# Where the fourth head's softmax denominator is summed: GpSimd adds in place of TensorE products with ones

## What is computed

```python
q = (x @ Wq.T).reshape(B, L, H, dh)
k = (x @ Wk.T).reshape(B, L, H, dh)
v = (x @ Wv.T).reshape(B, L, H, dh)
attn = jnp.einsum('blhd,bmhd->bhlm', q, k) / scale
p = jax.nn.softmax(attn, axis=-1)
o = jnp.einsum('bhlm,bmhd->blhd', p, v).reshape(B, L, D)
return o @ Wo.T
```

## Time and profile before

| | |
|---|---|
| median of three runs | 2779.42 us |
| lowest, highest | 2776.97, 2784.46 us |
| span of the profiled execution, first to last instruction | 2774.4 us |
| own time of the profiled execution | not given apart from its span |
| TensorE matmul busy | 2651.4 us, 96% |
| VectorE busy | 1546.9 us, 56% |
| ScalarE busy | 1295.4 us, 47% |
| GpSimd busy | 845.8 us, 30% |
| mean granted TensorE clock | 0.984 |

### The profile page before, as it was taken

One profiled execution on the slowest core, in us unless ns is written; L12 is line 12 of the kernel. 1 busy time (PEld: TensorE's weight loads), 2 busy tenths in 40 slices (PEclk: granted clock), 3 DMA queues, 4 the chain that ended last, 5 costly groups with the idle time before them and its releaser, 6 DMA issues. The chain is left out here.

```text
span 2774.4 us, 39374 instructions
## 1 busy us (share of the span) xinstructions
PE 2651.4 (96%) x11909; PEld 1714.2 (62%) x11909; DVE 1546.9 (56%) x2349; ACT 1295.4 (47%) x2274; POOL 845.8 (30%) x625
## 2 busy tenths in 40 slices
PE   6999999999999999999999987999999999999999
PEld 5644436544437444446444356888888888888887
DVE  4656754666745666636666535454545544545454
ACT  4355663455662555653556734433433343334333
POOL 0345552365560655632455522010101010101010
PEclk8999999999999999999999999999999999999999
DMA  5211213121103221132112153010101010101010
GB/s 176 56 35 39 47 42 97 35 46 50 54 18 91 47 48 49 43 88 54 36 39 46 43 189 137 1 46 1 47 1 46 1 47 1 46 1 47 1 46 16
DMA packets 66135, 135.34 MB, mean 49 GB/s; under 512 B 13668, under 2 KB 15720, under 8 KB 64616
## 3 DMA queue, kind: packets, MB, share of 16 engines
q1 hardware_dynamic: 64808, 128.24, 15.9%
q0 software_dynamic: 1088, 4.19, 0.4%
HBM read 59.78 MB, written 19.92 MB: 29 GB/s over the span
## 5 line engine op out<-in xcount | busy, mean ns | idle before, releaser
L577 DVE TENSOR_REDUCE pmax<-bank 128x1 f32<-128x512 f32 x1024 | 654.7, 683 | 353.3 <-PE bank L751 343.4
L501 ACT ACTIVATE probs<-bank 128x512 f32<-128x512 f32 x1024 | 581.2, 596 | 493.4 <-PE bank L816 479.5
L363 POOL TENSOR_TENSOR sums<-probs,sums 128x512 f32<-128x512 f32 x480 | 612.5, 1304 | 146.0 <-ACT probs L501 145.8
L816 PE MATMUL bank<-qs,ks 128*128 128x512 f32 x1024 | 456.0, 451 | 33.6 <-ACT probs L501 33.2
L816 PEld LDWEIGHTS bank<-qs,ks 128*128 128x128 f32 x1024 | 189.6, 188 | 380.0 <-issue 194.3
L751 PE MATMUL bank<-ks,qs 96*128 96x512 f32 x1024 | 401.6, 405 | 7.8 <-DVE pmax L577 7.5
L1382 PE MATMUL bank<-h_hi,gu_hi 128*128 128x512 f32 x1024 | 398.9, 390 | 7.3 <-DVE gu_lo L1247 5.4
L1382 PE MATMUL bank<-h_hi,gu_lo 128*128 128x512 f32 x1024 | 398.5, 389 | 0.0
L1382 PE MATMUL bank<-h_lo,gu_hi 128*128 128x512 f32 x1024 | 398.4, 389 | 0.0
L363 POOL TENSOR_TENSOR sums<-probs 128x512 f32<-128x512 f32 x96 | 120.8, 1285 | 683.2 <-ACT probs L501 458.1
L1275 DVE TENSOR_TENSOR sg<-bank,sg 128x512 f32<-128x512 f32 x128 | 88.4, 691 | 381.5 <-PE bank L1382 381.5
(11 more groups left out here) (123 smaller groups left out, 3145.8 us busy)
## 6 DMA issues: line engine op xcount, KB each, us to landing
ks<-qk_hi SPq DMA_DIRECT2D x136, 128.0 KB, 2.4
qs<-qk_hi SPq DMA_DIRECT2D x264, 64.0 KB, 2.0
x<-in_x SPq DMA_DIRECT2D x10, 1024.0 KB, 5.3
res<-in_x SPq DMA_DIRECT2D x9, 1024.0 KB, 5.3
x<-attn_out SPq DMA_DIRECT2D x9, 1024.0 KB, 7.5
ks<-qk_lo SPq DMA_DIRECT2D x68, 128.0 KB, 2.4
qs<-qk_lo SPq DMA_DIRECT2D x132, 64.0 KB, 2.0
wv<-wv_parts SPq DMA_DIRECT2D x4, 2048.0 KB, 8.6
```

Of the source, the lines that this page charges most:

```text
L363: nc.gpsimd.tensor_tensor(sums[:, h, :], probs[:, s % 2, h, :], before, ALU.add) \
L501: nc.scalar.activation(probs[:, s % 2, h, :], sbank[i % SB][:], ACT.Exp, scale=SCALE).then_inc(st_done, 1)
L577: nc.vector.reduce_max(pmax[:, t, h, hf:hf + 1], mbank[n % MB][:], AX_X).then_inc(sq_done, 1)
L816: nc.tensor.matmul(sbank[i % SB][:], ks[:, g % 2, h, s * P:(s + 1) * P], qs[:, u % 3, h, :], start=True, stop=True).then_inc(st_ready, 1)
```

## The change

`POOL_HEADS` is 4. POOL adds the exponentials of all four heads, 24 adds in a unit, and ACT's exponentials of head 3 wait for POOL like the others. PE's product of ones with head 3 is gone from key tiles 0 to 6; the last key tile keeps the products of all four heads, which now open the accumulation; `denominators` has four products in place of three. ACT copies `dbank` in one piece, in key tile 1. `den` moves to the place of the second half of `yout`, which adds two waits for results of earlier work (ACT before the first copy of a batch, DVE before the second output tile). Lines below 456 move by up to four.

```diff
-POOL_HEADS = 3
+POOL_HEADS = 4
...
-    sums = at("sums", [P, POOL_HEADS, QB], F32, "sums")
+    sums = at("sums", [P, GH, QB], F32, "sums")
...
+            def denominators(b, u):
+
+                act.wait_ge(d_ready, b * NU + (u + 2))
                 act.wait_ge(on_done, b * NU + (u + 1))
-                nc.scalar.activation(den[96:128, :], dbank[96:128, :], ACT.Copy).then_inc(od_act, 1)
-
-            def denominators(b, u):
-
-                act.wait_ge(d_ready, b * NU + (u + 2))
-                nc.scalar.activation(den[0:96, :], dbank[0:96, :], ACT.Copy).then_inc(od_act, 1)
+                if u == 0:
+
+                    act.wait_ge(y_stored[1], b * (NT // 2 * 16) + 16)
+                nc.scalar.activation(den[:], dbank[:], ACT.Copy).then_inc(od_act, 1)
...
-                            if h < POOL_HEADS and s != 1:
+                            if s != 1:
...
                     dve.wait_ge(y_stored[t % 2], b * (NT // 2 * 16) + (t // 2 + 1) * 16)
+                    if t == 1:
+
+                        dve.wait_ge(on_done, b * NU + NU + 1)
...
                 pe.wait_ge(sum_done, sums_done(b, u, NS - 2, POOL_HEADS - 1))
-                for h in range(POOL_HEADS):
+                for h in range(GH):
                     last = nc.tensor.matmul(dbank[DH * h:DH * h + DH, :], ones[:], sums[:, h, :], start=False, stop=True)
...
-                for h in range(0 if s == NS - 1 else POOL_HEADS, GH):
-                    last = nc.tensor.matmul(dbank[DH * h:DH * h + DH, :], ones[:], probs[:, s % 2, h, :],
-                                            start=(s == 0 or h < POOL_HEADS), stop=(s == NS - 1 and h >= POOL_HEADS))
+                    pe.wait_ge(od_act, b * (2 * NU) + (2 * u + 2))
+                    for h in range(GH):
+                        last = nc.tensor.matmul(dbank[DH * h:DH * h + DH, :], ones[:], probs[:, s % 2, h, :],
+                                                start=True, stop=False)
```

More of the change, by code:

```diff
@@ L444, in output @@
                 nc.scalar.activation(o[:, g, hf * QB:(hf + 1) * QB], obank[:], ACT.Copy).then_inc(od_act, 1)
-                act.wait_ge(on_done, b * NU + (u + 1))
-                nc.scalar.activation(den[96:128, :], dbank[96:128, :], ACT.Copy).then_inc(od_act, 1)
             def denominators(b, u):
                 act.wait_ge(d_ready, b * NU + (u + 2))
-                nc.scalar.activation(den[0:96, :], dbank[0:96, :], ACT.Copy).then_inc(od_act, 1)
+                act.wait_ge(on_done, b * NU + (u + 1))
+                if u == 0:
+                    act.wait_ge(y_stored[1], b * (NT // 2 * 16) + 16)
+                nc.scalar.activation(den[:], dbank[:], ACT.Copy).then_inc(od_act, 1)
             def output_hi(b, t):
@@ L597, in normalise @@
                 if part == 0:
-                    dve.wait_ge(od_act, b * (3 * NU) + (3 * (u + 1) + 2))
+                    dve.wait_ge(od_act, b * (2 * NU) + (2 * (u + 1) + 2))
                     link(nc.vector.transpose(den[:], den[:]))
@@ L766, in values @@
                 if s == 0:
-                    pe.wait_ge(od_act, b * (3 * NU) + (3 * u + 1))
+                    pe.wait_ge(od_act, b * (2 * NU) + (2 * u + 1))
                 for h in range(GH):
-                    nc.tensor.matmul(obank[DH * h:DH * h + DH, :], v[:, s, (g * GH + h) * DH:(g * GH + h + 1) * DH],
-                                     probs[:, s % 2, h, :], start=(s == 0), stop=(s == NS - 1))
+                    last = nc.tensor.matmul(obank[DH * h:DH * h + DH, :], v[:, s, (g * GH + h) * DH:(g * GH + h + 1) * DH],
+                                            probs[:, s % 2, h, :], start=(s == 0), stop=(s == NS - 1))
                 if s == NS - 1:
-                    pe.wait_ge(od_act, b * (3 * NU) + (3 * u + 2))
-                for h in range(0 if s == NS - 1 else POOL_HEADS, GH):
-                    last = nc.tensor.matmul(dbank[DH * h:DH * h + DH, :], ones[:], probs[:, s % 2, h, :],
-                                            start=(s == 0 or h < POOL_HEADS), stop=(s == NS - 1 and h >= POOL_HEADS))
+                    pe.wait_ge(od_act, b * (2 * NU) + (2 * u + 2))
+                    for h in range(GH):
+                        last = nc.tensor.matmul(dbank[DH * h:DH * h + DH, :], ones[:], probs[:, s % 2, h, :],
+                                                start=True, stop=False)
                 last.then_inc(pv_done, 1)
@@ L1422, in condition_block @@
         ("hT_hi", KT * L), ("hT_lo", KT * L), ("qk_hi", 2 * QB), ("qk_lo", 2 * QB), ("qs", 2 * GH * QB),
-        ("qs_2", GH * QB), ("ks", 2 * GH * L), ("v", NS * D), ("probs", 2 * GH * QB), ("sums", POOL_HEADS * QB), ("mt", TPH * P),
-        ("o", NG * L), ("den", QB), ("x4", TPH * D), ("yout", 2 * D), ("pmax", TPH * GH * NHALF),
+        ("qs_2", GH * QB), ("ks", 2 * GH * L), ("v", NS * D), ("probs", 2 * GH * QB), ("sums", GH * QB), ("mt", TPH * P),
+        ("o", NG * L), ("x4", TPH * D), ("yout", D), ("den", D), ("pmax", TPH * GH * NHALF),
         ("mx", TPH * GH), ("dsmall", QB // 32), ("indc", GH)])
```

## The result

The changed kernel takes 2823.39 us in the median of 4 runs (2798.65 to 2826.09), the kernel before, beside it on the same chip, 2778.19 us (2771.04 to 2784.46). The medians are 45 us apart, and the ratio of all runs is given as 1.0136, with an interval of 1.0093 to 1.018: it is slower. The forecast was 2623 us, and its range ended at 2680.

What follows compares the result with a forecast made beforehand. PE was taken to bound every unit. Units 0 to 5 gain 5.5 us each, unit 6 3.1, unit 7 2.9: 39.0 us a batch, 156 in four; 2779.4 - 156 = 2623 us, range 2580 to 2680.

Steps and rivals of the forecast that it cites:

- the rivals with slower adds: POOL adds at 1.45 us, time 2694, chance 0.04; or at 1.736 us, time 2890, chance 0.04.
- the one that gave a slower kernel: POOL becomes the bound with adds of 1.736 us, units of 45.0 us, time 2890; chance 0.04.
- The sum: Units 0 to 5: 6.65 - 0.95 - 0.25 - 0.3 + 0.35 = 5.5 us gained, so 36.9 us a unit.
- the growth of the maxima chain: Key tile 6, three small DVE operations PE waits for: the middle one lengthens, 0.25 us charged, bounds 0 and 0.9.
- 0.3 us for L608: Key tile 3, DVE's multiplication by the inverted denominator lengthens beside POOL's adds: 0.3 us charged, bounds 0 and 1.1.
- The rival with DVE starved: Unpausing POOL holds each maxima chain operation for a further add, 3.8 us more; gain 65 us, time 2715; chance 0.07.
- the prediction's own sign of being wrong: First adds 36.0 us or less apart, or 38 and more (adds over 1.4 us, or small DVE operations over 2).
- PE's 6.65 us a unit: Seven single products of ones removed from PE in a unit, 0.95 us each; 213 us in 32 units.
- The 0.35 us that the sum credits for ACT's copy: Key tile 1: ACT's 0.59 us copy of 32 partitions goes; 0.35 us credited, bounds 0 and 0.59.
- a gain of 3.1 us, to 34.4: Unit 6 taken as POOL-bound: 31.4 us of adds, 1.02 of inverse root, 1.95 of ACT, against 37.5 before.
- the root's 1.02 us on POOL: Unit 6: an inverse root on POOL, counted as 1.02 us beside the 24 adds.

Runs made afterwards that it cites:

- e10: Changed kernel, each POOL add waiting for the one before, unit 6's inverse root one key tile earlier, `mx` as a one-tensor reduction: 2641.58 us.
- e2: Kernel before without the single product of ones in key tiles 0 to 6, nothing in its place, POOL's 18 adds kept: 2665.26 us.
- e8: Kernel before without the single product of ones in key tiles 0 to 6, each POOL add waiting for the one before: 2632.5 us.
- e1: Changed kernel with every POOL add also waiting for the add right before it: 2676.96 us.

## Why the prediction was wrong

**What held.** The removed product stood on PE's path. The adds kept their pace, forecast 1.31 us and measured 1.27 in runs without a pause, so the rivals with slower adds are out, the one that gave a slower kernel too: it had the direction right by a cause that didn't come. ACT waits for POOL only 30 us in all, in 38 places. POOL isn't the bound of the changed kernel. In e10, with units of 37.27 us where the forecast had 36.9, it nearly is: units 0 to 3 of the second batch take 35.9 to 36.5 us, POOL adds for all but 3.0 to 3.6 us of each, and ACT waits for it for 99.7 us in 147 places.

**The step that failed: the price of DVE beside an unbroken POOL.** The sum charged 0.25 us for the growth of the maxima chain and 0.3 us for L608, with upper bounds of 0.9 and 1.1 us, read from the lengths before, which all end within one add. These bounds took the longest hold seen for the longest there is. The rival with DVE starved saw the place and still priced it at one further add for each operation, 3.6 us a unit, with a chance of 0.07. Measured is a hold of up to seven adds: (3620 - 1077) = 2.5 us a unit on the mean for the multiplication, and (1558 - 646) = 0.9 for `mx`. Units 0 to 5 take 44.5 us, which is the prediction's own sign of being wrong: 38 us and more with DVE operations over 2 us. What I missed is the ring. I had costed a DVE instruction as waiting for a given time; but POOL's run has no end of its own. It ends when ACT stops, which stops because PE does, which waits for the held DVE. Eleven adds in a row without a pause stood in the earlier trace rows, and I read them only as a pace for POOL, not as the length of time for which DVE can be shut out. No row of before shows such a hold, though: that adds in a row can shut DVE out past the first boundary only the changed kernel showed.

The Trainium skill, GPSIMD Engine Reference, Key points, states contention with DVE instructions in a two-port mode or with two SBUF inputs. The traces agree as far as they go: 680 ns with one operand in PSUM, 186 ns for the reduction, both beside adds. VectorE: DVE Perf Modes, What auto-detection actually checks, in the Trainium skill, gives a two-port mode to instructions with a single source and destination in SBUF, if their outermost dimensions are both even or equal and the firmware enables it for the operation; that can put L591 among the held ones, and there it was, 4464 ns on the mean. Neither page says that the contention can last over many adds.

**The second step: PE's saving.** The sum gave PE's 6.65 us a unit back but for the chain. By e2 and e8 it is worth 116 to 118 us, 3.7 us a unit, even with nothing added to POOL. I had checked one key tile, where ACT stood idle for 1.85 us, and took from it that ACT has room everywhere. But PE already waited for a score bank in 332 places, 167.8 us in all, and I hadn't read that row; a PE that comes earlier waits there in more places, 438 in e2. The maxima banks, the chain and the clock take the rest (above). The 0.35 us that the sum credits for ACT's copy were not measured apart.

**Unit 6.** Forecast was a gain of 3.1 us, to 34.4. The forecast counted the root's 1.02 us on POOL, but not who waits for it: DVE and PE, behind 16 adds. With that mended it takes 36.3 us.

**The clock.** The forecast had no term for it. The changed kernel's clock over 100 to 1500 us is 0.92 on the mean, e10's 0.99, and the timeline showed it at the lower level behind the stall. Between 100 and 1500 us it is at the lower level for 233 us, in e1 for 82. So part of the loss is PE at half speed, and the rows give its size as an estimate. In the attention PE is busy at the lower level for 212 us here and for 65 in e1; half of the difference, 73 us, is the most that this adds. PE's waits for DVE at the maxima products (L755) and the chain's products (L741) are 161 us here and 48 in e1 (L753, L739), 113 us more. Together that is more than the 153 us between the two spans, in part because e1 waits longer elsewhere, 31.4 against 18.6 us for the scaled x. How they divide exactly isn't shown. No run held the clock fixed.

**Together.** 2641.6 us in e10 is 19 us from the forecast of 2623, but by other terms: less from PE, and 24 gaps a unit. That the two times are near each other is partly luck. The forecast described a kernel in which POOL's runs can be broken; the change as written doesn't do that.

**What stays open.** What lets a DVE instruction in at one boundary and not at the next. The two multiplications shown began 0.56 and 0.55 us into an add (counted from the single records); the first was held over seven adds, the second let in at once. So the place within the add alone doesn't decide. The gap makes the boundary safe, and it is argued, not shown, that 0.1 us of pause is what does it. The Trainium skill, GPSIMD Engine Reference, Instruction dispatch, says that each of POOL's cores starts the next instruction as soon as its own share is done, unless a semaphore holds it back. By that, back-to-back adds leave no moment in which all of POOL is off the shared interface; the traces agree in that the records of such adds overlap by 0.04 us, while those with the wait stand 0.08 us apart. It can't be the whole of it, since most DVE instructions are let in at the first boundary of adds whose records overlap. A changed kernel without gaps and with no instruction of that kind at all in DVE's attention wasn't tried.

## What to carry to other kernels

Before work is moved to GpSimd, list the VectorE instructions that will run beside it and share its interface, and ask what ends GpSimd's run: if it is the engine that waits for VectorE, the hold can last until GpSimd's input is used up. A wait of each GpSimd instruction on the one before it cost 0.1 us each here and was worth 146 us, and 33 us even in the kernel before. The time that an operation takes on a busy engine is an upper bound of what its removal is worth; count the waits just behind it (here for two score banks), since they take up part of what is freed; here 45% was lost, to these waits, the maxima chain and the clock together.

## What was unexpected of the hardware

- A DVE instruction of 16 elements a partition, 175 ns by itself, took up to 9.4 us beside back-to-back GpSimd adds; one of 512 elements a partition up to 8.6 us, 0.69 by itself.
- A hold ends either at the first boundary between two adds or with the run: all 76 holds of over 2 us ended with POOL's run.
- Taking away one held instruction moved the hold to the next one, nearly unchanged in size (151.6 and 142.8 us in all), even to one that reads a single tensor.
- Reading one operand from PSUM, or reducing over a pair in place of a two-tensor maximum, isn't held: 680 and 186 ns on the mean, 689 and 189 at most, in 32 units each.
- 0.1 us of pause between adds makes GpSimd 9% slower (1.26 to 1.37 us an add) and the kernel 5% faster.
